# The gated recurrence of a decoder kernel: four time steps per round in place of one

## The reference, cut to what matters

```python
def _L1_attn_ref(x, omega, Win, Wl, bl, Wv, bv, Wout):
    xz = jnp.einsum('btd,ed->bte', x, Win)
    xi, z = jnp.split(xz, 2, axis=-1)               # 256 features each
    log_lam = -C * jax.nn.softplus(omega) * jax.nn.sigmoid(jnp.einsum('bti,ji->btj', xi, Wl) + bl)
    lam = jnp.exp(log_lam)
    v = jnp.einsum('bti,ji->btj', xi, Wv) + bv
    h0 = xi[:, 0]
    def step(h_prev, inp):
        x_t, v_t, lam_t = inp
        vh = jnp.sum(v_t * h_prev, axis=-1, keepdims=True)
        vv = jnp.sum(v_t * v_t, axis=-1, keepdims=True)
        Qh = h_prev - 2.0 * v_t * (vh / vv)
        h = lam_t * Qh + (1.0 - lam_t) * x_t
        return (h, h)
    ...                                              # scan over t = 1 .. 127
    return jnp.einsum('bti,di->btd', jax.nn.silu(z) * h, Wout)
```

## Time and profile before

| what | us |
|---|---|
| median of 3 runs | 1151.41 (1149.92 to 1156.63) |
| the profiled execution | 1156.96 |
| its span | 1155.1 |
| DVE busy in it | 887.1 (77%) |
| TensorE busy in it | 984.8 (85%) |
| POOL busy in it | 357.0 (31%) |
| recurrence, from its first L864 to the first L885 | 603.45 to 742.73 |

### The profile page before, as it was taken

The page is one execution under the profiler, slowest core; times in us unless marked ns, Lnnn a source line. Parts: engine busy times, 40 slices in busy tenths (PEclk is TensorE's granted clock), DMA queues, the critical chain, the costliest instruction groups (busy, mean ns, idle before and its releaser), DMA issues.

```text
span 1155.1 us, 15884 instructions
## 1 busy us (share of the span) xinstructions
PE 984.8 (85%) x5754; PEld 734.3 (64%) x5754; DVE 887.1 (77%) x1860; ACT 524.4 (45%) x884; POOL 357.0 (31%) x428
## 2 busy tenths in 40 slices
PE   6766767676779999998869999889996899999998
PEld 4222222222558888885428888857664779999997
DVE  6689999999775555562868888868997468887886
ACT  5564544454254222236720000055664556667774
POOL 6175666666320101110752222254442001001110
PEclk9879989899987999998985555578999899999999
DMA  6000000000000100100000000000000000000001
GB/s 168 1 0 0 1 0 1 0 0 1 1 1 1 28 15 28 46 20 0 1 0 1 1 1 1 1 0 2 3 2 1 1 2 19 19 20 19 20 19 38
DMA packets 19865, 13.87 MB, mean 12 GB/s; under 512 B 3067, under 2 KB 18313, under 8 KB 19786
## 3 DMA queue, kind: packets, MB, share of 16 engines
q1 hardware_dynamic: 19786, 12.84, 3.9%
HBM read 11.79 MB, written 1.05 MB: 11 GB/s over the span
## 4 chain that ended last, share of the span: by engine, by line
PE 51%; DVE 16%; ACT 4%; issue 2%; POOL 1%; DVEq 0%; ACTq 0%
PE ps L1025 18%; PE ps L1019 15%; PE ps L1223 6%; DVE small L903 2%; PE ps L1185 2%; DVE G L906 2%; PE ps L1325 1%; DVE lm L860 1%; PE ps L1267 1%; DVE rrec L866 1%; PE ps L1216 1%; DVE G L870 1%; DVE stats L615 1%; DVE sdot L864 1%; ACT G L569 1%
## 5 line engine op out<-in xcount | busy, mean ns | idle before, releaser
L1025 PE MATMUL ps<-xhl,whl 128*128 128x512 f32 x960 | 251.1, 412 | 12.9 <-DVE xhl L632 6.7
L1025 PEld LDWEIGHTS ps<-xhl,whl 128*128 128x128 f32 x960 | 182.1, 196 | 53.0 <-issue 12.0
L294 POOL TENSOR_TENSOR R<-G,R 128x1024 f32<-128x1024 f32 x64 | 150.6, 2355 | 105.8 <-DVE R L722 77.5
L722 DVE TENSOR_TENSOR_SCAN R<-ps,R 128x1024 f32<-128x1024 f32 x64 | 146.4, 2289 | 7.7 <-ACT ps L460 5.8
L1223 PE MATMUL ps<-lm,ones 128*128 128x16 f32 x504 | 126.1, 376 | 12.5 <-DVE lm L860 11.0
L1223 PEld LDWEIGHTS ps<-lm,ones 128*128 128x128 f32 x504 | 115.3, 318 | 24.8 <-DVE lm L860 19.5
L1078 PE MATMUL ps<-R,ident 128*128 128x512 f32 x256 | 127.2, 621 | 0.0
L1019 PEld LDWEIGHTS ps<-R,G 128*128 128x128 f32 x1024 | 119.0, 192 | 6.4 <-DVE G L949 4.1
L1019 PE MATMUL ps<-R,G 128*128 128x128 f32 x1024 | 119.7, 275 | 3.1 <-DVE G L949 3.1
L587 ACT ACTIVATE G<-ps,w_exp_bi 128x512 f32<-128x512 f32 x128 | 90.0, 703 | 65.9 <-PE ps L1025 54.9
L1061 PE MATMUL ps<-bc,sel 96*128 96x512 bf16 x128 | 50.2, 408 | 81.0 <-DVE R L738 68.8
(11 more groups left out here) (220 smaller groups left out, 1557.0 us busy)
## 6 DMA issues: line engine op xcount, KB each, us to landing
ew<-in_w_dram SPq DMA_DIRECT2D x24, 128.0 KB, 2.4
R<-in_exp_wi_dram SPq DMA_DIRECT2D x8, 256.0 KB, 2.8
R<-in_exp_wo_dram SPq DMA_DIRECT2D x8, 256.0 KB, 3.2
X<-in_x_dram SPq DMA_DIRECT2D x4, 256.0 KB, 3.9
out_dram<-X SPq DMA_DIRECT2D x4, 256.0 KB, 2.3
w_ctxT<-in_ctxT_dram SPq DMA_DIRECT2D x1, 487.5 KB
ew<-in_sw_dram SPq DMA_DIRECT2D x3, 128.0 KB, 2.1
w_W_in<-in_W_in_dram SPq DMA_DIRECT2D x1, 256.0 KB, 4.8
```

The lines of the kernel that those rows point to most:

```text
L294: gp.tensor_tensor(dBu[:, j, :].rearrange("p (h n) -> p h n", h=HI), duT[:, :, gcols(g)], Bsb[:, i % 4:i % 4 + 1, :].broadcast_to([P, HI, ...
L722: v.tensor_tensor_scan(hst[:, j, :], bank(2 * j, 2).rearrange("p h n -> p (h n)"), dBu[:, j, :], 0.0, ALU.mult, ALU.add).then_inc(S["scann ...
L1025: ins = mm(out, whl[:, wslot(n), i, m * P:(m + 1) * P], xhl[:, j, gcols(g)], start=k == 0, stop=k == 2)
```

## The change

Four steps become one round. Within a chunk of four tokens the four dot products depend on the state at the chunk's start and on each other through a 4 x 4 lower triangular system, whose coefficients are six dot products per chunk (`PAIRS`). They are computed in the preparation for all chunks at once. POOL forms the products over features (`kp`, placed in `ew0`) and the vectors `wc` (placed in `xi`) that carry each dot product to the end of its chunk. DVE multiplies the lams of a chunk (`chunk_products`), scans the state as it would be without the dot products (`state_without_dots`), and `solve` runs the elimination on vectors (`U`) and constants (`cp`). TensorE sums over features in `chunk_dots`; ACT copies in `carry_last` and `e_copy`. Positions of a chunk are addressed by `pos`: columns 16 bytes apart.

The recurrence has 32 rounds. DVE multiplies the chunk's `U` by the incoming state (L955), TensorE sums (L1339) on top of the known part (`s_known`, L1326), DVE multiplies `wc` by the result (L959) and reduces it with the carried state (L957, L963). ACT copies the dot products out (L601), POOL multiplies `ww` by them and subtracts `nb` for spans of up to eight chunks (`DRIVES`; L362, L365), and after the last round eight scans of 512 columns give all states. POOL gates the first three groups, DVE the last. SP loads the last block's experts after this gating, because `R` is in use until then.

The diff, cut to its core; removed are `shift_v`, L316 to L334, L854 to L885 and L1210 to L1227 of the kernel before:

```diff
+C4 = 4
+NC = T // C4
+KG = GB * NC
+PAIRS = ((1, 0), (2, 1), (3, 2), (2, 0), (3, 1), (3, 0))
+DRIVES = (0, 8, 16, 24, 30, 32)
...
+        kp = ew0[:].rearrange("p s w n -> p (s w n)").rearrange("p (h j k) -> p h j k", h=HI, k=KG)
+        ep, hp = (R[:, 0, i, :].rearrange("p (h n) -> p h n", h=HI) for i in range(2))
...
-            sp.wait_ge(S["y_gated"], NG)
+            sp.wait_ge(S["g1_ready"], NG - 1)
+            sp.wait_ge(S["g1_last"], 1)
...
+            gp.memset(eb[:, :, :, 0:1], 0.0)
+            for g in range(NG):
+                L, V, W, C = (pos(buf, g) for buf in (lam, vv, ww, wc))
+                pool.wait_ge(S["nb_done"], g + 1)
+                pool.wait_ge(S["w_done"], g + 1)
+                if g:
+                    pool.wait_ge(S["kd_mm"], g)
+                gp.tensor_tensor(kp[:, :, 0:3], V[:, :, 1:4], W[:, :, 0:3], ALU.mult).then_inc(S["k_in"], 1)
+                step(gp.tensor_tensor(C[:, :, 0:3], L[:, :, 1:4], W[:, :, 0:3], ALU.mult))
+                gp.tensor_tensor(kp[:, :, 3:5], V[:, :, 2:4], C[:, :, 0:2], ALU.mult).then_inc(S["k_in"], 1)
+                pool.wait_ge(S["k_in"], 3 * g + 2)
+                step(gp.tensor_tensor(C[:, :, 0:2], L[:, :, 2:4], C[:, :, 0:2], ALU.mult))
+                gp.tensor_tensor(kp[:, :, 5], V[:, :, 3], C[:, :, 0], ALU.mult).then_inc(S["k_in"], 1)
+                pool.wait_ge(S["k_in"], 3 * g + 3)
+                gp.tensor_tensor(C[:, :, 0], L[:, :, 3], C[:, :, 0], ALU.mult).then_inc(S["wc_done"], 1)
+                pool.wait_ge(S["hp_done"], HI * (g + 1))
+                if g:
+                    pool.wait_ge(S["ed_mm"], g)
+                gp.tensor_tensor(eb[:, :, :, 1:T], tok(vv, g)[:, :, :, 1:T], hb[:, :, :, 0:T - 1], ALU.mult).then_inc(S["e_in"], 1)
+                pool.wait_ge(S["e_in"], g + 1)
+                pool.wait_ge(S["pl_done"], g + 1)
+                gp.tensor_tensor(V[:, :, 1], V[:, :, 1], L[:, :, 0], ALU.mult)
+                gp.tensor_tensor(V[:, :, 2], V[:, :, 2], prod[:, g % 2, 0], ALU.mult)
+                gp.tensor_tensor(V[:, :, 3], V[:, :, 3], prod[:, g % 2, 1], ALU.mult).then_inc(S["vp_done"], 1)
+            span = lambda buf, c0, c1: buf.rearrange("p h (b t) -> p h b t", b=B)[:, :, :, C4 * c0:C4 * c1]
+            for k in range(len(DRIVES) - 1):
+                c0, c1 = DRIVES[k], DRIVES[k + 1]
+                pool.wait_ge(S["s_copied"], c1)
+                d = span(ww, c0, c1)
+                gp.tensor_tensor(d, d, s_sb[:, :, C4 * c0:C4 * c1].unsqueeze(1).broadcast_to([P, HI, B, C4 * (c1 - c0)]),
+                                 ALU.mult).then_inc(S["ws_done"], 1)
+                pool.wait_ge(S["ws_done"], k + 1)
+                gp.tensor_tensor(d, d, span(nb, c0, c1), ALU.subtract).then_inc(S["drive1"], 1)
+            for g in range(NG - 1):
+                pool.wait_ge(S["h_scan"], HI * (g + 1))
+                pool.wait_ge(S["z_silu"], HI)
+                gp.tensor_tensor(nb[:, :, gcols(g)], vv[:, :, gcols(g)], z1[:, :, gcols(g)], ALU.mult).then_inc(S["g1_ready"], 1)
...
+            def carry_last(g):
+                act.wait_ge(S["w_done"], g + 1)
+                sc.copy(pos(wc, g)[:, :, 3], pos(ww, g)[:, :, 3]).then_inc(S["w3_done"], 1)
+            def e_copy(g):
+                act.wait_ge(S["ed_mm"], g + 1)
+                sc.copy(cp[:, gcols(g)], bank(6)[:, 0, :]).then_inc(S["e_ev"], 1)
...
+            act.wait_ge(S["vv_mm"], NG)
+            for c in range(NC):
+                act.wait_ge(S["s_mm"], c + 1)
+                if c < NC - 1:
+                    act.wait_ge(S["r_w"], 2 * c + 2)
+                sc.copy(s_sb[:, :, C4 * c:C4 * c + C4], slot(c).rearrange("p (b i) -> p b i", i=C4)).then_inc(S["s_copied"], 1)
...
+            def chunk_products(g):
+                L = pos(lam, g)
+                if g >= 2:
+                    dve.wait_ge(S["vp_done"], g - 1)
+                step(v.tensor_tensor(prod[:, g % 2, 0], L[:, :, 0], L[:, :, 1], ALU.mult))
+                step(v.tensor_tensor(prod[:, g % 2, 1], prod[:, g % 2, 0], L[:, :, 2], ALU.mult))
+                v.tensor_tensor(carry[:, :, g * KG:(g + 1) * KG], prod[:, g % 2, 1], L[:, :, 3], ALU.mult).then_inc(S["pl_done"], 1)
+            def state_without_dots(g):
+                dve.wait_ge(S["nb_done"], g + 1)
+                if g:
+                    dve.wait_ge(S["e_in"], g)
+                for h in range(HI):
+                    v.tensor_tensor_scan(hp[:, h, :], lam[:, h, gcols(g)], nb[:, h, gcols(g)], 0.0, ALU.mult, ALU.add)\
+                        .then_inc(S["hp_done"], 1)
+            def solve(g):
+                dve.wait_ge(S["kd_mm"], g + 1)
+                dve.wait_ge(S["vp_done"], g + 1)
+                dve.wait_ge(S["e_ev"], g + 1)
+                U = pos(vv, g)
+                c_i = cp[:, gcols(g)].rearrange("p (k i) -> p i k", i=C4)
+                for j, (b, first) in enumerate(((4, 0), (5, 0), (5, 2))):
+                    n, done = 3 - j, 3 * g + j
+                    kj = bank(b)[:, 0, first * KG:(first + n) * KG].rearrange("p (i k) -> p i k", k=KG)
+                    if done:
+                        dve.wait_ge(S["u_done"], done)
+                        dve.wait_ge(S["c_done"], done)
+                    v.tensor_tensor(u_tmp[:, :, 0:n], kj.unsqueeze(1).broadcast_to([P, HI, n, KG]),
+                                    U[:, :, j:j + 1, :].broadcast_to([P, HI, n, KG]), ALU.mult).then_inc(S["u_mul"], 1)
+                    v.tensor_tensor(c_tmp[:, 0:n], kj, c_i[:, j:j + 1, :].broadcast_to([P, n, KG]), ALU.mult).then_inc(S["c_mul"], 1)
+                    dve.wait_ge(S["u_mul"], done + 1)
+                    v.tensor_tensor(U[:, :, j + 1:4], U[:, :, j + 1:4], u_tmp[:, :, 0:n], ALU.add).then_inc(S["u_done"], 1)
+                    dve.wait_ge(S["c_mul"], done + 1)
+                    v.tensor_tensor(c_i[:, j + 1:4], c_i[:, j + 1:4], c_tmp[:, 0:n], ALU.add).then_inc(S["c_done"], 1)
...
+                chunk_products(g)
...
+                state_without_dots(g)
+                if g >= 2:
+                    solve(g - 2)
+            solve(NG - 2)
+            solve(NG - 1)
...
+            for c in range(NC):
+                h_in = hc_in[:, c % 2].unsqueeze(3)
+                if c:
+                    dve.wait_ge(S["r_h"], c)
+                v.tensor_tensor(uh[:, c % 2], chunk(vv, c), h_in.broadcast_to([P, HI, B, C4]), ALU.mult).then_inc(S["r_q"], 1)
+                if c < NC - 1:
+                    v.tensor_tensor(ws[:, c % 2, :, :, C4:C4 + 1], chunk_carry(c), h_in, ALU.mult).then_inc(S["r_w"], 1)
+                    dve.wait_ge(S["s_mm"], c + 1)
+                    v.tensor_tensor(ws[:, c % 2, :, :, 0:C4], chunk(wc, c),
+                                    slot(c).rearrange("p (b i) -> p b i", i=C4).unsqueeze(1).broadcast_to([P, HI, B, C4]),
+                                    ALU.mult).then_inc(S["r_w"], 1)
+                    dve.wait_ge(S["r_w"], 2 * c + 2)
+                    v.tensor_reduce(hc_in[:, (c + 1) % 2], ws[:, c % 2], AX.X, ALU.add).then_inc(S["r_h"], 1)
+            dve.wait_ge(S["drive1"], len(DRIVES) - 1)
+            for g in range(NG):
+                for h in range(HI):
+                    v.tensor_tensor_scan(vv[:, h, gcols(g)], lam[:, h, gcols(g)], ww[:, h, gcols(g)], 0.0, ALU.mult, ALU.add)\
+                        .then_inc(S["h_scan"], 1)
+            dve.wait_ge(S["h_scan"], HI * NG)
             dve.wait_ge(S["z_silu"], HI)
-            for g in range(NG):
-                v.tensor_tensor(nb[:, :, gcols(g)], xi[:, :, gcols(g)], z1[:, :, gcols(g)], ALU.mult).then_inc(S["g1_ready"], 1)
+            last = gcols(NG - 1)
+            v.tensor_tensor(nb[:, :, last], vv[:, :, last], z1[:, :, last], ALU.mult).then_inc(S["g1_last"], 1)
...
+            def chunk_dots(g):
+                pe.wait_ge(S["k_in"], 3 * (g + 1))
+                if g == 0:
+                    pe.wait_ge(S["xz_ev"], 4 * NG)
+                else:
+                    pe.wait_ge(S["u_mul"], 3 * g)
+                    pe.wait_ge(S["c_mul"], 3 * g)
+                for n, (i, j) in enumerate(PAIRS):
+                    b, first = ((4, 0), (5, 0), (5, 2))[j]
+                    o = first + i - j - 1
+                    for k in range(HI):
+                        ins = mm(bank(b)[:, 0, o * KG:(o + 1) * KG], ones[:], kp[:, k, n, :], start=k == 0, stop=k == HI - 1)
+                ins.then_inc(S["kd_mm"], 1)
+                pe.wait_ge(S["e_in"], g + 1)
+                if g:
+                    pe.wait_ge(S["e_ev"], g)
+                for k in range(HI):
+                    ins = mm(bank(6)[:, 0, :], nones[:], ep[:, k, :], start=k == 0, stop=k == HI - 1)
+                ins.then_inc(S["ed_mm"], 1)
...
+            def s_known(c):
+                if c >= 4:
+                    pe.wait_ge(S["s_copied"], c - 3)
+                mm(slot(c), ident[:], cp.rearrange("p (b t) -> p b t", b=B)[:, :, C4 * c:C4 * c + C4], start=True, stop=False,
```

(47 more changed lines are left out.)

107 lines of the change are left out of this document (37 added, 70 removed).

## The result

The changed kernel took 1190.39 us (median of 4 runs, 1189.27 to 1193.13), beside 1151.43 us (1149.92 to 1156.63) for the one before: ratio 1.033, 95% interval 1.030 to 1.037. It is slower. The forecast was 1167 us, so the sign was right and the size was not: 39 us measured, 15.5 forecast. The profiled executions took 1189.66 and 1156.96 us and their spans differ by 32.8 us; the profiled run of the kernel before lay 5.5 us above its median. Most of that arose ahead of the changed code, as the next rows show.

The account below looks back on a forecast made before the run. Low-clock TensorE and DVE were both nearly full in the recurrence, with latency the cost. Preparation +58.7, recurrence -56.0 and the end +12.8 gave +15.5 us: 1172.5 profiled, 1167 as median; 8 in 10 for 1128 to 1197.

Parts of the forecast that it names:

- Preparation: Per-token vectors in four groups ahead of the recurrence: 25.1 us a group plus 13 us waits, recurrence starting 58.7 us later.
- I take 2.19: POOL's products in the preparation: 2.19 ns an element, from contiguous rows, with 3.35 at most from a strided row.
- I take 13 us for all waits: Preparation: time that neither DVE's nor POOL's turns fill, such as `kp`, banks and last solves; ends 3 and 30.
- DVE's strides: DVE on columns 16 bytes apart in the preparation: 0.6 ns more, 1.65 ns an element, with 0 and 1.0 as ends.
- Turns: DVE operations with two SBUF inputs and POOL operations exclude each other, so their times add: 25.1 us a preparation group.
- Recurrence: 127 steps (139.3 us) become 32 rounds of 2.24 us plus 11.6 us for drive operations, 83.3 in all: -56.0 us.
- Behind it: After the recurrence: scans, gatings and residual adds; 19.4 us where 5.0 stood before, less 1.6 at the adds: +12.8 net.
- The -1.6 us for the adds: Four residual adds at the end: the fourth comes 6.6 us behind the first in place of 8.2.
- The first, POOL's strides: Preparation: strided POOL operations at 3.35 ns an element cost 18 us more, total 1185; chance 0.20.
- The second (no turns): Preparation, rounds and end: new forms do not take turns with POOL, sum -23 us, total 1128; chance 0.23.
- the third: Recurrence: TensorE gets 2.4 GHz, -16 us, total 1151, no change; chance 0.15.

Follow-up runs that it names:

- experiment 1: Changed kernel with POOL's preparation products and ACT's carry copy on contiguous quarters instead of columns 16 bytes apart (other values): 1174.0 us, ratio 1.018.
- experiment 3: Changed kernel with the sums of odd groups in PSUM banks 0 and 1, waiting for `solve` of two groups back: 1177.38 us, ratio 1.022.
- Experiments 6 and 7: Each on the changed kernel: three gatings moved from POOL to DVE, 1187.93 us; POOL's drive operations on four-chunk spans timed to fit between turns, 1184.53 us.

## Why the size was wrong, step by step

- **Preparation, +58.7 forecast, +84.4 measured.** The failed step has two terms. "I take 2.19" for POOL: both inputs strided, it is 3.75 ns an element. With the rows of 1.15, 2.11 and 3.07 us (three, two and two of them), two of 0.85 and L350's 2.33, POOL's group is 17.8 us in place of 12.2, 22 in four groups; experiment 1 takes 17.3 us off the stage. "I take 13 us for all waits": neither POOL nor a DVE operation with two SBUF inputs is at work for 25.5 us, and experiment 3 takes 12.7 off the stage with a second set of banks. Counted so, the 25.7 us too few divide about evenly: the time in which one of the two is at such work is 113.4 us for 100.4 forecast, the rest 25.5 for 13. The first is less than the full 22 of POOL's strides, because beside strided operations of POOL the turns cost somewhat less than the full sum; by how much is not worked out here. The text named the wait for `kp` and for the banks and then priced only the last two solves, as if POOL's wait in the groups between were covered by turns; the idle rows say it wasn't.
- **DVE's strides, 1.65 ns an element forecast.** The timeline of DVE in three of the solves:
```profile
602.67 1.47 DVE L917 TENSOR_TENSOR R<-ps,G 128x768 f32<-128x768 f32 x1
...
604.79 1.50 DVE L921 TENSOR_TENSOR G<-G,R 128x768 f32<-128x768 f32 x1
...
610.28 0.60 DVE L917 TENSOR_TENSOR R<-ps,G 128x256 f32<-128x256 f32 x1
...
655.97 2.93 DVE L921 TENSOR_TENSOR G<-G,R 128x768 f32<-128x768 f32 x1
...
674.15 1.51 DVE L917 TENSOR_TENSOR R<-ps,G 128x768 f32<-128x768 f32 x1 [3.84 <-ACT R L563]
...
683.24 0.37 DVE L923 TENSOR_TENSOR R<-R 128x128 f32<-128x128 f32 x1
```
L917 took 1.47 us at 768 elements and 0.60 at 256: 1.70 ns an element. Right, but partly by luck: the row of TensorE that the prediction used as a neighbour (L1216, 7.14 us) does not read columns 16 bytes apart. Its innermost step goes from one sequence to the next, 128 elements or 512 bytes, and so does that of the strided inputs at L860, L866 and L331. None of the rows that the prediction used had steps of 16 bytes. The last `solve`, alone, took 9.5 us (674.15 to 683.61) for 8.7.
- **Turns.** Right, for strided forms too: L921 takes 1.50 us alone and 2.93 at 655.97, while POOL's second product of 768 runs. Experiments 6 and 7 confirm it at the scans and at the drive operations.
- **Recurrence, -56.0 forecast, some -61 measured** (80.3 us up to the first scan, of which 2.0 belong to the end). Two rows of DVE's timeline around a drive operation:
```profile
699.47 0.29 DVE L955 TENSOR_TENSOR R<-G,hc_in 128x128 f32<-128x128 f32 x1
...
701.64 2.46 DVE L955 TENSOR_TENSOR R<-G,hc_in 128x128 f32<-128x128 f32 x1
...
705.99 0.56 DVE L955 TENSOR_TENSOR R<-G,hc_in 128x128 f32<-128x128 f32 x1
```
A round is 2.17 us (2.24 forecast), the product that meets POOL's L362 takes 2.46 in place of 0.29, and all such delays make 9 us (11.6 forecast).
- **Behind it.** Eight scans beside the gatings took 15.34 us for 16.2 forecast. From the last round to the first residual add it is 18.5 us for 19.4 forecast, 5.0 before. The -1.6 us for the adds did not come: the fourth stands 8.15 us behind the first, as before. Net about +13.5 for 12.8. The scans took turns, which the forecast had left open between 0 and 7.1 and taken as 7.1.
- **Rivals.** The first, POOL's strides, was right in kind and near in price: 17 us by experiment 1, 18 forecast, where I had thought 3.35 ns unlikely. Its sum of 1185 lies 5 below the measured time and kept the 13 us for waits. It should have been the main case: the only strided row of POOL said 267 ns for 32 elements, and I set it aside because 32 elements are few. The Trainium skill (GPSIMD Engine Reference, the section on performance pitfalls for Q7 kernels) speaks of half as much again for reads over 8 bytes apart; here it was 70% more (3.75 for 2.19), and the measurement decides. The second (no turns) and the third (clock; it stayed at 0.50) did not occur.
